# Attention on one Trainium2 core: pairwise maxima and the norm's scale kept in spare columns of the score banks

## The reference

```python
# every layer: x = x + layer(layernorm(x))
qkv = x @ W_qkv                                   # 16 heads of 8 channels
ql = jnp.einsum('bhtd,hdr->bhtr', q, W_q_lsr)     # rank 32
kl = jnp.einsum('bhsd,hdr->bhsr', k, W_k_lsr)
scores = jnp.einsum('bhtr,bhsr->bhts', ql * lsr_core[None, :, None, :], kl) * scale
scores = jnp.where(causal[None, None], scores, -jnp.inf)
attn = jax.nn.softmax(scores, axis=-1)
y = jnp.einsum('bhts,bhsd->bhtd', attn, v)
return y.transpose(0, 2, 1, 3).reshape(b, t, d) @ W_o
```

## Time and profile before

| | us |
|---|---|
| median of 3 runs | 2399.09 (2396.4 to 2400.65) |
| span of the profiled execution, first to last instruction | 2296.9 |
| VectorE busy | 1880.2 (82%) |
| TensorE busy | 1602.6 (70%) |
| ScalarE busy | 1471.2 (64%) |
| POOL busy | 1394.7 (61%) |

### The profile page before, as it was taken

How to read it: one execution, slowest core, us unless ns; L and a number is a source line. 1 busy time by engine, 2 the same in 40 slices (tenths; PEclk the granted TensorE clock), 3 DMA queues, 4 the chain that set the end, 5 groups by cost and what they waited for, 6 DMA issues and landing times. The chain is left out here.

```text
span 2296.9 us, 52136 instructions
## 1 busy us (share of the span) xinstructions
PE 1602.6 (70%) x16780; PEld 1341.8 (58%) x16780; DVE 1880.2 (82%) x4914; ACT 1471.2 (64%) x3849; POOL 1394.7 (61%) x1494
## 2 busy tenths in 40 slices
PE   4667576675765469994788888888886747999000
PEld 2445445454445349993577777777785626998000
DVE  6999999999997878885899999999994797888122
ACT  5666676676753468883588887887886276887000
POOL 3545555555550037774599888888886006775776
PEclk8777777787875679997899999999998568999555
DMA  1000101001035013343112211221111402334222
GB/s 29 15 14 14 28 15 28 14 15 28 14 93 141 20 37 94 94 90 61 33 51 57 57 53 50 55 56 53 54 45 40 127 1 66 94 94 83 71 79 72
DMA packets 188967, 122.59 MB, mean 53 GB/s; under 512 B 24321, under 2 KB 177825, under 8 KB 188705
## 3 DMA queue, kind: packets, MB, share of 16 engines
q1 hardware_dynamic: 154016, 75.18, 11.7%
q0 software_dynamic: 17408, 35.69, 7.1%
q10 hardware_dynamic: 17280, 8.40, 1.3%
HBM read 66.22 MB, written 44.04 MB: 48 GB/s over the span
## 5 line engine op out<-in xcount | busy, mean ns | idle before, releaser
L1044 POOL DMA_INDIRECT ffn_xs<-normed,ffn_tokeni x288 | 320.8, 1114 | 349.4 <-DVE posi L1420 262.2
L1858 POOL TENSOR_TENSOR att_pl<-att_p,att_ph 128x384 f16<-128x384 f32 x512 | 462.2, 922 | 87.8 <-ACT att_ph L2079 78.6
L323 POOL TENSOR_TENSOR sq<-states,qS 128x256 f32<-128x256 f32 x256 | 250.7, 979 | 304.6 <-DVE states L733 303.7
L543 ACT ACTIVATE decayed<-states,alpha 128x64 f32<-128x64 f32 x1024 | 272.2, 336 | 177.7 <-DVE states L733 175.8
L379 PE MATMUL bank<-sq,ident 128*128 128x128 f32 x1024 | 250.0, 415 | 92.9 <-POOL sq L323 92.9
L2176 DVE TENSOR_REDUCE att_mx<-bank 128x3 f32<-128x384 f32 x512 | 276.1, 549 | 39.2 <-PE bank L1915 35.7
L2076 ACT ACTIVATE att_p<-bank 128x384 f32<-128x384 f32 x512 | 251.6, 491 | 84.3 <-PE bank L1952 79.9
L379 PEld LDWEIGHTS bank<-sq,ident 128*128 128x128 f32 x1024 | 220.6, 241 | 128.2 <-POOL sq L323 100.2
L1251 ACT ACTIVATE ffn_h<-bank,b_cols 128x256 f32<-128x256 f32 x576 | 225.8, 474 | 61.2 <-PE bank L1139 59.7
L2079 ACT ACTIVATE att_ph<-bank 128x384 f16<-128x384 f32 x512 | 252.2, 493 | 0.0
L1439 DVE TENSOR_TENSOR ffn_hl<-ffn_h,ffn_hh 128x512 f16<-128x512 f32 x288 | 199.7, 693 | 39.2 <-ACT ffn_hh L1260 34.3
(11 more groups left out here) (333 smaller groups left out, 5116.6 us busy)
## 6 DMA issues: line engine op xcount, KB each, us to landing
slots<-ffn_ys SPq DMA_DIRECT2D x144, 128.0 KB, 2.2
ffn_x_all<-x SPq DMA_DIRECT2D x16, 512.0 KB, 4.8
normed<-ffn_xn ACTq DMA_DIRECT2D x32, 256.0 KB, 2.3
att_qz<-att_qp SPq DMA_DIRECT2D x256, 32.0 KB
ffn_xs<-normed,ffn_tokeni POOLq DMA_INDIRECT x288
xin<-in_x SPq DMA_DIRECT2D x64, 64.0 KB, 2.0
xres<-in_x SPq DMA_DIRECT2D x64, 64.0 KB, 2.0
x<-x SPq DMA_DIRECT2D x64, 64.0 KB, 1.7
```

What stands on the lines that cost most here:

```text
L323: nc.gpsimd.tensor_tensor(sq[:, t, :].rearrange("p (h i j) -> p h i j", h=HL, i=D), states[:, t, :].rearrange("p (h i j) -> p h i j", h=HL ...
L543: ins = nc.scalar.activation(decayed[:, 64 * h:64 * h + 64], states[:, (t - 1) % TC, 64 * h:64 * h + 64], ACT.Copy, scale=alpha[p][:, t, h ...
L1044: pool.indirect_dma_start(xs[j % AHEAD][:, r, :], None, A["normed"], bass.IndirectOffsetOnAxis(ap=tokeni[:, BR * j + r:BR * j + r + 1], ax ...
L1858: nc.gpsimd.tensor_tensor(pl[:, h % RP, :], p32[:, h % RP, :], ph[:, h % RP, :], ALU.subtract).then_inc(low_done, 1)
```

## The change

The score banks have 128 columns that no score uses. The change puts two things there.

`larger` becomes a reduction over pairs that writes 16 numbers to columns 392 to 407 of score bank 1, and `high` and `low` read them there. For that `mx` gets a fourth number per head, cleared once to -3e38 on POOL, so that both token blocks are a maximum over a pair. Since the bank is in use meanwhile, the maxima of heads 9 and 15 no longer release it: they raise `maxi_dve`, and `low0` or `low1` raises `max_done` in their place.

For batches 3 to 31 a new operation `scale` copies `rstd` to columns 384 and 385 of score bank 0, and `xn0`, `xn1` read it there, as a three-input operation in place of a two-scalar one. They stand directly behind the maxima of head 12, which no longer release the bank; `xn1` does. Whoever waited for `xn1` on `front_dve` now waits on `max_done`. In the prologue (batch 0) the maxima's small operations stand behind their heads, instead of behind all sixteen.

```diff
+SCALE_AT = SW
+LARGER_AT = SW + 8
+HELD = {9: "maxima0", 15: "maxima1"}
+XN_AT = FRONT_DVE_AT["xn0"]
-MAXI = list(MAXI_FIRST_AT) + list(MAXI_SECOND_AT)
+FRONT_DVE_HELD = [n for n in FRONT_DVE if n not in ("xn0", "xn1", "x_low")] + ["scale", "xn0", "x_low"]
+MAXI = ["maxima0", "larger0", "high0", "rows0", "maxima1", "larger1", "high1", "rows1"]
...
-        mx = [sb(f"mx{p}", [P, H, 3]) for p in range(2)]
+        mx = [sb(f"mx{p}", [P, H, 4]) for p in range(2)]
...
+        def xn_written(eng, b):
+            if b < 3:
+                eng.wait_ge(front_dve, front_at(b, "xn1"))
+            else:
+                eng.wait_ge(max_done, (b - 2) * H + XN_AT + 1)
+
+        def maxima_split(eng, b, n):
+            eng.wait_ge(max_done, b * H + sorted(HELD)[n] + 1)
...
+                for p in range(2):
+                    pool.memset(mx[p][:, :, 3], -3e38).then_inc(ready, 1)
...
-                pe.wait_ge(front_dve, at(FRONT_DVE, b, "xn1"))
+                xn_written(pe, b)
...
-                pe.wait_ge(maxi_dve, at(MAXI, b, f"low{n}"))
+                maxima_split(pe, b, n)
...
                 elif name.startswith("xn"):
-                    dve.wait_ge(front_act, at(FRONT_ACT, b, "rstd"))
+                    if b < 3:
+                        dve.wait_ge(front_act, at(FRONT_ACT, b, "rstd"))
+                    else:
+                        dve.wait_ge(front_dve, front_at(b, "scale"))
+                        ins = v.scalar_tensor_tensor(xn[:, k, :], xin[p % 2][:, k, :], mv[:, k, 0:1],
+                                                     ps_s[XN_AT % 2][:, SCALE_AT + k:SCALE_AT + k + 1].to_broadcast([P, E]),
+                                                     ALU.subtract, ALU.mult)
+                        ins.then_inc(front_dve if k == 0 else max_done, 1)
+                        return
...
+                elif name == "scale":
+                    dve.wait_ge(front_act, at(FRONT_ACT, b, "rstd"))
+                    ins = v.tensor_reduce(ps_s[XN_AT % 2][:, SCALE_AT:SCALE_AT + TB], rstd[:, :].unsqueeze(2), AX_X, ALU.max)
...
-                v.tensor_reduce(mx[p % 2][:, h, :], ps_s[h % 2][:, 0:SW].rearrange("p (a n) -> p a n", n=P), AX_X,
-                                ALU.max).then_inc(max_done, 1)
+                ins = v.tensor_reduce(mx[p % 2][:, h, 0:3], ps_s[h % 2][:, 0:SW].rearrange("p (a n) -> p a n", n=P), AX_X,
+                                      ALU.max)
+                if h in HELD:
+                    ins.then_inc(maxi_dve, 1)
+                elif not keep:
+                    ins.then_inc(max_done, 1)
...
-                m = mx[p % 2][:, HH * n:HH * n + HH, :]
+                m = mx[p % 2][:, HH * n:HH * n + HH, :].rearrange("p h (k j) -> p k h j", j=2)
+                larger = ps_s[sorted(HELD)[n] % 2][:, LARGER_AT:LARGER_AT + TB * HH].rearrange("p (k h) -> p k h", k=TB)
                 if name[:-1] == "larger":
-                    dve.wait_ge(max_done, b * H + HH * (n + 1))
-                    ins = v.tensor_tensor(m[:, :, 0], m[:, :, 0], m[:, :, 1], ALU.max)
+                    dve.wait_ge(maxi_dve, at(MAXI, b, f"maxima{n}"))
+                    ins = v.tensor_reduce(larger, m, AX_X, ALU.max)
...
-                    ins = v.tensor_scalar(mrow[n][:, :, :, 3 * D], m[:, :, 0:3:2].rearrange("p h k -> p k h"),
+                    ins = v.tensor_scalar(mrow[n][:, :, :, 3 * D], larger,
                                           -(2.0 ** (-2 * AS)), None, ALU.mult)
...
-                    ins = v.scalar_tensor_tensor(mrow[n][:, :, :, 3 * D + 1], m[:, :, 0:3:2].rearrange("p h k -> p k h"),
-                                                 -(2.0 ** (-2 * AS)), mrow[n][:, :, :, 3 * D], ALU.mult, ALU.subtract)
+                    v.scalar_tensor_tensor(mrow[n][:, :, :, 3 * D + 1], larger, -(2.0 ** (-2 * AS)), mrow[n][:, :, :, 3 * D],
+                                           ALU.mult, ALU.subtract).then_inc(max_done, 1)
+                    return
...
                     if later(i, p, 1):
-                        maxima(*later(i, p, 1), h)
+                        maxima(*later(i, p, 1), h, keep=bool(h == XN_AT and later(i, p, 3)))
+                    if later(i, p, 3) and h == XN_AT:
+                        for name in ("scale", "xn0", "xn1"):
+                            front(name, *later(i, p, 3))
...
                         for name in FRONT_DVE:
-                            if FRONT_DVE_AT[name] == h:
+                            if FRONT_DVE_AT[name] == h and name[:2] != "xn":
                                 front(name, *later(i, p, 3))
```

More of the change, by code:

```diff
@@ L1708, in at, with front_at @@
             return b * len(names) + names.index(name) + 1
+        def front_at(b, name):
+            return at(FRONT_DVE if b < 3 else FRONT_DVE_HELD, b, name)
+        def xn_written(eng, b):
[5 more added lines that the diff above has]
+            eng.wait_ge(max_done, b * H + sorted(HELD)[n] + 1)
         def proj_at(b, name):
@@ L1743, in load @@
                 if not under(b, 2):
-                    sp.wait_ge(front_dve, at(FRONT_DVE, b - 2, "xn1"))
+                    xn_written(sp, b - 2)
                     ii, pp = sooner(i, p, 2)
@@ L1757, in keep @@
                 b = NBUF * i + p
-                sp.wait_ge(front_dve, at(FRONT_DVE, b, "add11"))
+                sp.wait_ge(front_dve, front_at(b, "add11"))
                 sp.dma_start(midb[b], xin[p % 2][:, :, :]).then_inc(x_mid[p % 2], 16)
@@ L1791, in _ @@
             place(0, 0, 0)
-            sp.wait_ge(ready, 2 + 2 + 2 * NBUF)
+            sp.wait_ge(ready, 2 + 2 + 2 + 2 * NBUF)
             sp.wait_ge(cleared, 3)
@@ L1832, in take_places @@
                 if not under(b, 2):
-                    pool.wait_ge(front_dve, at(FRONT_DVE, b - 2, "add11"))
+                    pool.wait_ge(front_dve, front_at(b - 2, "add11"))
                 t = b * TB
@@ L1883, in proj @@
                 if name == "q01":
-                    pe.wait_ge(front_dve, at(FRONT_DVE, b, "x_low"))
+                    pe.wait_ge(front_dve, front_at(b, "x_low"))
                 elif name == "q23":
@@ L1997, in _ @@
                 s_pass(0, 0, h)
-            pe.wait_ge(ready, 2 + 2 + 2 * NBUF)
+            pe.wait_ge(ready, 2 + 2 + 2 + 2 * NBUF)
             turn_max(0, 0, 0)
@@ L2041, in front @@
                 if name == "rstd_log":
-                    act.wait_ge(front_dve, at(FRONT_DVE, b, "aggr1"))
+                    act.wait_ge(front_dve, front_at(b, "aggr1"))
                     ins = a(lnv[:, :], mv[:, :, 1], ACT.Ln, bias=eps[:, :])
@@ L2095, in _ @@
                 front(name, 0, 2)
-            act.wait_ge(ready, 2 + 2 + 2 * NBUF)
+            act.wait_ge(ready, 2 + 2 + 2 + 2 * NBUF)
             def step(i, p):
@@ L2128, in front @@
                     else:
-                        dve.wait_ge(front_dve, at(FRONT_DVE, b, f"add0{t}"))
+                        dve.wait_ge(front_dve, front_at(b, f"add0{t}"))
                     tile = b * TB + t
@@ L2135, in front @@
                 elif name.startswith("stats"):
-                    dve.wait_ge(front_dve, at(FRONT_DVE, b, f"add1{k}"))
+                    dve.wait_ge(front_dve, front_at(b, f"add1{k}"))
                     ins = v.bn_stats(st[:, k, :], xin[p % 2][:, k, :])
                 elif name.startswith("aggr"):
-                    dve.wait_ge(front_dve, at(FRONT_DVE, b, f"stats{k}"))
+                    dve.wait_ge(front_dve, front_at(b, f"stats{k}"))
                     dve.sem_inc(stats_seen, 1)
@@ L2171, in proj, with maxima @@
                 ins.then_inc(proj_dve, 1)
-            def maxima(i, p, h):
+            def maxima(i, p, h, keep=False):
                 b = NBUF * i + p
                 dve.wait_ge(s_ps, b * H + h + 1)
-                v.tensor_reduce(mx[p % 2][:, h, :], ps_s[h % 2][:, 0:SW].rearrange("p (a n) -> p a n", n=P), AX_X,
-                                ALU.max).then_inc(max_done, 1)
+                ins = v.tensor_reduce(mx[p % 2][:, h, 0:3], ps_s[h % 2][:, 0:SW].rearrange("p (a n) -> p a n", n=P), AX_X,
[4 more added lines that the diff above has]
+                    ins.then_inc(max_done, 1)
             def maxi(name, i, p):
@@ L2234, in _ @@
             v.memset(qz[3][:, :, :, :], 0.0).then_inc(cleared, 1)
-            dve.wait_ge(ready, 2 + 2 + 2 * NBUF)
+            dve.wait_ge(ready, 2 + 2 + 2 + 2 * NBUF)
             for h in range(H):
                 maxima(0, 0, h)
-            for name in MAXI_FIRST_AT:
-                maxi(name, 0, 0)
+                for name in MAXI_FIRST_AT:
+                    if MAXI_FIRST_AT[name] == h and name != "rows0":
+                        maxi(name, 0, 0)
+            maxi("rows0", 0, 0)
             for name in FRONT_DVE:
```

## The result

The changed kernel takes 2343.89 us in the median (2342.5 to 2345.13), the kernel before 2399.31 beside it: a ratio of 0.9771, with a 95% interval of 0.9759 to 0.9783, or 55.4 us less. The forecast was 2366 us with 2350 as the lower end, so the change brought more than the range allowed. Three executions that lie far off the others of their kernel (2620.9 us of e3, 3146.07 and 2366.13 us of the kernel before) are left out of the ratios.

What follows compares the result with a forecast made beforehand. TensorE and VectorE handing over bound the attention loop, POOL close behind. TensorE's 1.75 us saving, limited by POOL, took the period from 20.62 to 19.55 us; times 31, 33 us off 2399.1 gave 2366 us, range 2350 to 2390.

Steps and rivals of the forecast that it cites:

- 102.2 us lie around the span: Whole kernel: median 2399.09 us less span 2296.9 us, taken as time outside the span that the change doesn't touch.
- the allowance of 0.2 to 0.3 us: Attention, per batch: left for engines that hand over to each other, giving a period of 19.55 us.
- POOL's floor: Attention: POOL's instructions without waits take 19.36 us per batch, or 19.13 with 0.23 us won on the subtractions.
- The wait for `xn`: TensorE's wait for `xn1` in each attention period: 0.80 us, to fall by 0.46 to 0.34.
- The wait for `low0`: TensorE's wait for the first half's `low` in each attention period: 1.01 us, to fall by 0.73 to 0.28.
- The two behind `low1`: TensorE's waits of 0.33 and 0.38 us per attention period, both to go as `low1` comes 1.33 us sooner.
- The new wait in front of head 1's pass: Attention: head 15's held bank delays the next batch's score pass of head 1, costing TensorE 0.15 us.
- VectorE's busy time: Attention, per batch: 19.46 us, to fall by 1.33, 0.73 and 0.46 to 16.94 us.
- rival A: POOL's blocking moves to the additions of the experts' rows; gain only 19 us, 2380 us; chance 0.25.
- B: Rival: POOL's floor is lower and all waits vanish, period 19.1 us, gain 47 us, 2352 us; chance 0.08.
- C: Rival: operations writing SBUF wait for POOL whatever they read, and head 15's held bank costs; 42 us slower, 2441; chance 0.07.
- D: Rival: changed operations get short, but other hand-overs take the time back; within 5 us of before; chance 0.08.

Runs made afterwards that it cites:

- e3: Changed kernel with its order and holds, but `larger` and `rstd` read from SBUF; 2324.59 us against 2298.15 for the kernel before, ratio 1.0116.
- e6: Kernel before with POOL's subtraction cut from 384 to 8 columns; 2345.18 us against 2399.18 for the kernel before.
- e0: Kernel before, run once more unchanged; 2296.78 us against 2298.15 for the kernel before beside it.
- e5: Kernel before, unchanged, traced in a job of the long case; 2397.03 us in a single execution.
- e11: Changed kernel with `rows0` on VectorE in slot 10 instead of 11; 2254.42 us against 2254.65 for the changed kernel.
- e12: Changed kernel with POOL's subtraction cut to 8 columns and `rows0` in slot 10; 2243.32 us against 2298.55 for the kernel before.
- e7: Changed kernel with POOL's subtraction cut from 384 to 8 columns; 2358.2 us, ratio 0.9831 to the kernel before.
- e10: Kernel before with only the norm's part of the change (`scale`, `xn0`, `xn1`, head 12 held); 2297.8 us, ratio 0.9992.
- e9: Kernel before with only the maxima's part (`larger`, `high`, `low`, heads 9 and 15 held); 2308.03 us, ratio 1.0042.
- e15: Changed kernel without POOL's copy of places, first two additions in slot 2 instead of 1; 2393.52 us against 2299.79 for the kernel before.

## Why the prediction was wrong

**The mechanism was right.** Operations of VectorE with two SBUF inputs or in the form of `high` and `xn` wait for POOL, and with a bank as an input they don't. e3 and e6 show it from both sides: `high` takes 0.832 us in the median from SBUF and 0.228 from the bank beside the same subtractions, and 0.203 from SBUF with POOL's work cut short. This agrees with what the Trainium skill says in "GPSIMD Engine Reference", "Key points". That the wait ends with the instruction that POOL is running holds for the earlier trace rows, but not always (see the last section). Durations: `high` and `low` 0.23 us for 0.20 forecast, `larger` 0.18 to 0.20 for 0.20, `scale` and both `xn` 0.15 + 0.61 for 0.80. The higher price for a bank that the Trainium skill gives ("VectorE: DVE Perf Modes", the errata section, 62 cycles or 65 ns more) doesn't show in that size: in the median `high` takes 228 ns from the bank and 203 from SBUF undisturbed (e6), `low` 229 and 229. An `xn` takes 344 and 340, but those are two forms of the instruction.

**First failed step: "102.2 us lie around the span".** They don't (e0, e5). The trace was of the short case, the median of the long one. I took the period of 20.62 us to be that of the timed kernel; that one had 21.04, and 0.42 x 31 = 13 us of gain were missing from the sum. A gap of 4% between span and time should have been a warning: after the change it is 1.7 us.

**Second: the allowance of 0.2 to 0.3 us for two engines that "don't both stay full", and the rounding up to 19.55.** POOL's floor was 19.13 us by my own sum, and the period is 19.16: POOL does reach its floor. The difference to 19.55 is 0.39 x 31 = 12 us. That POOL can stay full because the product with the values runs four heads behind is my reading, which no run tests. The prologue and the last batch gave 4 us back (54.4 us instead of 31 x 1.88 = 58.3), which makes 21 of the 22 us of the miss. For the short case, whose trace I had, the same working would have said 2299 - 33 = 2266 us; it is 2254.65, so there the second step alone makes the miss.

**TensorE's terms.** The wait for `xn`, forecast 0.34, is 0.33. The wait for `low0`, forecast 0.28, is 0.49. The two behind `low1` are gone, as forecast. The new wait in front of head 1's pass, forecast 0.15, doesn't show, since TensorE comes there later for another wait that I didn't look for: the DMA behind `rows0`, 0.61 us. Without that one it is there, with 0.2 us (e11, e12). The DMA's wait is harmless here (e11) and costs when POOL doesn't bind (e7, e10). I had put the way from `rows0` to its reader at nothing, without a reason. So 1.43 us of waits are left instead of my 0.28 + 0.34 + 0.15 = 0.77.

**VectorE's busy time** I put at 16.94 us; it is 281.52 / 300 x 19.16 = 17.98. More than half of the difference is rival A: the additions have a mean of 528 ns between 1300 and 1600 us now, where the kernel before has 375, so 4 x 0.153 = 0.6 us per batch. Rival A therefore did occur, at less than half of its full size of 1.4 us, and cost nothing that shows, since VectorE had room and POOL was the bound. B was near the truth with its 19.1 us and its 2352; it had 0.08. C was refuted; e3 shows the cost of its held bank only for operations that still read SBUF. D was refuted.

**What I did not see at all** is that the parts don't add. By my sum the maxima's part was worth 1.29 us per batch and the norm's 0.46; measured alone they are worth -0.3 and 0 us by the time. The sum took each wait of TensorE as if the others stayed where they were. In e9 the saving went into a longer wait for `xn`, in e10 into the DMA behind `rows0`. That 1.26 to 1.49 us of it could be kept with both parts together is therefore partly luck: I had no argument for why these two moves would be missing there.

**What stays open.** Why a job falls into the long or the short case (no run here varies that; in the expert layers it shows as idle time of TensorE, for the larger part without a releaser in the profile), and why the clock granted in e9's attention is 0.97.

## What to carry to other kernels

When VectorE and POOL both work on SBUF, look for small operations of VectorE whose durations have a minimum far below the median, and hold their ends against the ends of POOL's instructions: if they agree, a bank as the source takes them out. Don't add up what each move should bring: in this periodic loop a saved wait came back at the next operation that POOL blocks (e9) or at a DMA (e10), and a change of one slot cost more (e15) than the whole repair brings. Run the parts alone as well as together. And check that span and median time belong together before a difference is worked out from a trace.

## What the runs showed of the hardware that I had not expected

A blocked operation of VectorE doesn't always get in at the next boundary between two instructions of POOL. The first `xn` of the pair in e9 (2.372 us) and the first addition of the pair in e15 (3.412 us) came through only when POOL had no subtraction left in the row, past at least two boundaries between subtractions of 0.88 us; the second of each pair then took 0.33 and 0.34 us. In the earlier trace rows `high` and `low` each wait for one instruction of POOL only. What decides between the two forms no run shows.

The same program on the same chip took 2399.2 us in one job and 2299.8 us in another. Of the 100 us between the spans of e5 and e0, 35 lie in each of the two expert layers, 12 in the attention and 12 behind the very last addition of the kernel (from there to the end of the span 6.5 us in e0 and 18.1 in e5).
